# A decoder layer on one core: the twelve sign-weight loads move from SyncE's queue to ScalarE's, under new orders for all engines

## What is computed

```python
# causal self-attention, 16 heads of width 32
Q, K, V = X @ Wq.T + bq, X @ Wk.T + bk, X @ Wv.T + bv
attn = softmax(where(causal, Q @ K.T * scale, -inf))
x = layernorm(x + (attn @ V) @ Wo.T + bo)
# cross-attention: the rows of x are mixed by an attention of ctx with itself
q, k = ctx @ Wxq.T + bxq, ctx @ Wxk.T + bxk
x = layernorm(x + x @ softmax(q @ k.T).T)
# ternary feed-forward, hidden width 2048
xq = round(127 / max|n(x)| * n(x)) * max|n(x)| / 127     # n: row normalisation
x = layernorm(x + (silu(xq @ sign(W_g).T) * (xq @ sign(W_u).T)) @ sign(W_d).T)
```

## Time and profile before

| what | us |
|---|---|
| median of 3 runs (646.59 to 647.51) | 647.17 |
| span of the profiled execution | 649.9 |
| PE busy | 610.3 (94%) |
| DVE busy | 527.2 (81%) |
| ACT busy | 417.9 (64%) |
| POOL busy | 340.8 (52%) |
| chain that ended last: PE's share | 62% |

### The profile page before, as it was taken

How to read it: one execution, slowest core, us unless ns; L and a number is a source line. 1 busy time by engine, 2 the same in 40 slices (tenths; PEclk the granted TensorE clock), 3 DMA queues, 4 the chain that set the end, 5 groups by cost and what they waited for, 6 DMA issues and landing times.

```text
span 649.9 us, 14332 instructions
## 1 busy us (share of the span) xinstructions
PE 610.3 (94%) x5356; PEld 417.1 (64%) x5356; DVE 527.2 (81%) x1376; ACT 417.9 (64%) x789; POOL 340.8 (52%) x472
## 2 busy tenths in 40 slices
PE   5995798998999999999899999999999999999996
PEld 4572476665766677757466666777776667676563
DVE  5786575996998976669999998758998899897775
ACT  6838597954667886635574795754467568963341
POOL 9236554421663784435882465533577337736253
PEclk9998697998999999999999999999999999999999
DMA  9885512062011210151200030111222010010000
GB/s 313 276 284 163 197 68 50 24 234 89 14 32 43 75 35 2 25 163 38 61 11 2 17 115 3 26 26 66 50 50 50 18 50 3 2 37 30 1 33 33
DMA packets 31461, 45.63 MB, mean 70 GB/s; under 512 B 5664, under 2 KB 22560, under 8 KB 29856
## 3 DMA queue, kind: packets, MB, share of 16 engines
q1 hardware_dynamic: 30848, 44.20, 21.8%
q10 hardware_dynamic: 544, 0.52, 0.2%
HBM read 27.79 MB, written 4.19 MB: 49 GB/s over the span
## 4 chain that ended last, share of the span: by engine, by line
PE 62%; DVE 11%; ACT 6%; issue 4%; SPq 1%; POOL 1%; DMA 1%; POOLq 0%; ACTq 0%; DVEq 0%
PE ps_b L672 20%; PE ps_b L840 15%; PE ps_b L855 14%; PE ps_b L767 4%; PE ps_b L746 3%; PE ps_b L776 2%; DVE ps_b L1118 1%; PE ps_b L729 1%; ACT ph L949 1%; PE ps_b L725 1%; SPq L634 1%; ACT ps_b L950 1%; DVE qk L1100 1%; ACT p L936 1%; DVE dg L1211 1%
## 5 line engine op out<-in xcount | busy, mean ns | idle before, releaser
L1118 DVE CUSTOM_DVE_ANT_0 ps_b<-ps_b,future 128x256 f32<-128x256 f32 (+3 forms) x256 | 118.9, 515 | 17.7 <-PE ps_b L725 11.3
L1319 POOL TENSOR_TENSOR ph<-p,ph 128x512 f16<-128x512 f32 x96 | 110.3, 1165 | 42.2 <-ACT ph L873 41.5
L840 PE MATMUL ps_b<-xqT,sg 128*128 128x256 f16 x1024 | 124.3, 275 | 3.8 <-ACT xqT L873 2.4
L855 PE MATMUL ps_b<-sd,hp 128*128 128x512 fp8e4 x512 | 119.1, 379 | 0.0
L1315 POOL TENSOR_TENSOR hp<-gt,hp 128x512 f16<-128x512 f32 x64 | 74.1, 1164 | 82.7 <-ACT hp L873 82.7
L840 PEld LDWEIGHTS ps_b<-xqT,sg 128*128 128x128 fp8e4 x1024 | 99.4, 98 | 22.5 <-issue 4.1
L1277 POOL TENSOR_SCALAR_AFFINE_SELECT p<-p 128x256 f32<-128x256 f32 (+1 forms) x96 | 46.5, 494 | 77.8 <-ACT p L936 77.0
L672 PE MATMUL ps_b<-xhl,wh 128*128 128x256 f16 x480 | 82.4, 273 | 0.0
L855 PEld LDWEIGHTS ps_b<-sd,hp 128*128 128x128 f16 x512 | 48.7, 98 | 51.1 <-POOL hp L1315 0.3
L1028 ACT ACTIVATE gt<-gt 128x512 f32<-128x512 f32 x64 | 40.1, 629 | 47.0 <-DVE gt L1226 46.9
L936 ACT ACTIVATE p<-ps_b 128x512 f32<-128x512 f32 x96 | 54.2, 598 | 19.3 <-PE ps_b L746 18.5
(11 more groups left out here) (135 smaller groups left out, 1208.2 us busy)
## 6 DMA issues: line engine op xcount, KB each, us to landing
st<-qk SPq DMA_DIRECT2D x192, 64.0 KB, 2.0
hp<-in_sgT_dram SPq DMA_DIRECT2D x6, 1024.0 KB, 7.2
gt<-in_sgT_dram SPq DMA_DIRECT2D x6, 1024.0 KB, 6.5
rows<-in_x_dram SPq DMA_DIRECT2D x8, 512.0 KB, 3.7
out_dram<-rows SPq DMA_DIRECT2D x16, 256.0 KB, 2.0
xin<-in_xT_dram SPq DMA_DIRECT2D x14, 256.0 KB, 3.5
e<-in_ctxT_dram SPq DMA_DIRECT2D x4, 512.0 KB, 4.1
hp<-in_wT_dram SPq DMA_DIRECT2D x4, 256.0 KB, 4.4
```

Source lines behind the costliest of these rows:

```text
L840: ins = pe.matmul(ps[:, a * HALF:(a + 1) * HALF], sg[:, ("gg", "uu").index(name), c, ht * P:(ht + 1) * P], xqT[:, c, :], start=c == 0, sto ...
L855: ins = pe.matmul(ps[:, :], hp[:, (UNITS * s + n) % HP_SLOTS, h, a, t * P:(t + 1) * P], sd[:, ht, :], start=ht == h == 0, stop=ht == HT - ...
L1118: ins = dve.tensor_tensor_reduce(scores, scores, future[:, S - width:S], 1.0, -3e38, ALU.add, ALU.max, tops[:, g // 2, j:j + 1, g % 2, qt ...
L1319: pool.tensor_tensor(out_, in_, hi, ALU.subtract).then_inc(signal, 1)
```

## The change

It does five things. `load_signs` leaves the sync engine and is issued by ScalarE, with the same waits (`w_lo` for the first two, then the sign of piece i - 2), now held by ScalarE. All five tables and the banks are written anew. Words of single steps take the place of pairs. GpSimd's `rms_scale` waits for the root that `row_scale` just made. The functions are otherwise as they were.

```diff
-            def load_signs(i):
-                if i < 2:
-                    sp.wait_ge(w_lo, 4 * (i + 1))
-                else:
-                    sp.wait_ge(signs, i - 1)
-                sp.dma_start(stage[i % 2], sgT[i]).then_inc(weight_in[i % 2], 16)
...
+            def load_signs(i):
+                if i < 2:
+                    wait_for(act, w_lo, 4 * (i + 1))
+                else:
+                    wait_for(act, signs, i - 1)
+                act.dma_start(stage[i % 2], sgT[i]).then_inc(weight_in[i % 2], 16)
...
             def rms_scale(s, t):
                 tile = 2 * (s % 2) + t
                 root = rstd[:, 1, tile:tile + 1]
+                wait(pool, ln_rstd[1], s, t + 1)
```

Two lines of the tables for scale, on TensorE, where `mx1.0.0.0` is the first product that needs `sk1.0.0.*`:

```diff
-st0.1.2.2@0 qk1.0.3@3 mx1.0.0.0@5 en0.3@4 pv0.1.1.0@6 pv0.1.1.1@6 pv0.1.1.2@6 pv0.1.1.3@6 st0.1.2.3@0 st0.1.2.4@7
...
+st0.1.2.5@6 op0.0.0@5 mx1.0.0.1@0 mx1.0.0.0@4 pv0.1.2.0@2 st0.1.2.3@7 tx0.0.0@5 op0.0.1@4 pv0.1.2.1@2 ta0.2@5
```

More of the change, by code:

```diff
@@ L130 @@
[L130 to L144, removed]
@@ new lines @@
+pv0.1.1.3@4 st0.1.3.0@0 st0.1.3.2@1 st0.1.2.4@2 to0.0.1@7 st0.1.2.5@6 op0.0.0@5 mx1.0.0.1@0 mx1.0.0.0@4 pv0.1.2.0@2
+st0.1.2.3@7 tx0.0.0@5 op0.0.1@4 pv0.1.2.1@2 ta0.2@5 pv0.1.2.2@2 st0.1.3.3@6 tx0.0.1@4 ta0.3@7 pv0.1.2.3@2 st0.1.3.1@1
+st0.1.3.4@3 mx1.0.0.2@5 st0.1.3.6@0 st0.1.3.5@1 xm0.0.0@7 xm0.0.1@6 pv0.1.3.0@7 pv0.1.3.1@7 pv0.1.3.2@7 pv0.1.3.3@7
+va1.0.0@6 to0.1.0@7 to0.1.1@0 mx1.0.1.1@1 mx1.0.3.0@2 va1.0.1@4 mx1.0.2.1@6 op0.1.0@7 ib0@4 mx1.0.1.0@0 op0.1.1@5
+mx1.0.2.0@1 mx1.0.1.2@0 mx1.0.2.2@4 tq0.0.0@7 qk1.1.0@3 qk1.1.1@1 nm1.0.0@3 tq0.0.1@2 tx0.1.1@4 mx1.0.3.2@6
@@ new lines @@
+mx1.0.3.1@7 tx0.1.0@0 uu0.0.1@2 gg0.0.0@3 uu0.0.0@7 xm0.1.0@4 st1.0.0.0@3 xm0.1.1@6 mx1.1.0.1@3 mx1.1.0.4@4
+mx1.1.0.0@7 gg0.0.2@0 gg0.0.1@6 mx1.1.0.2@1 uu0.0.3@5 uu0.0.2@3 qk1.1.2@7 mx1.1.0.3@0 st1.0.0.2@6 gg0.0.3@1 cp1.0@3
+cp1.1@4 mx1.1.0.5@7 st1.0.0.1@0 st1.0.1.0@2 gg0.0.5@3 gg0.0.4@7 mx1.1.0.6@4 mx1.1.1.0@6 gg0.0.6@2 mx1.1.0.7@5
+mx1.1.1.1@0 uu0.0.4@1 en1.0@5 uu0.0.5@6 pv1.0.0.0@0 dn0.0.1.0@7 mx1.1.1.2@5 st1.0.1.1@4 en1.1@1 pv1.0.0.1@0
+pv1.0.0.2@0 pv1.0.0.3@0 ta1.0@5 st1.0.1.2@4 qk1.1.3@3 dn0.0.0.0@5 ta1.1@0 mx1.1.1.3@4 mx1.1.1.4@1 mx1.1.1.6@6
@@ new lines @@
+dn0.0.0.1@5 pv1.0.1.0@0 dn0.0.0.2@5 gg0.0.7@2 uu0.0.6@1 ib1@4 mx1.1.1.5@3 pv1.0.1.1@0 pv1.0.1.2@0 pv1.0.1.3@0
+mx1.1.2.0@1 nm1.0.1@4 dn0.0.1.1@7 tq0.1.1@0 uu0.0.7@4 tq0.1.0@2 mx1.1.2.1@6 mx1.1.1.7@3 dn0.0.1.2@7 st1.0.2.0@1
+st1.0.2.1@0 nm1.1.0@6 en1.2@2 mx1.1.3.3@1 mx1.1.2.2@3 en1.3@6 mx1.1.2.3@0 st1.0.2.2@4 dn0.0.0.3@5 gg0.1.0@0 ta1.2@4
+st1.0.3.1@6 mx1.1.2.5@5 st1.1.0.2@2 mx1.1.2.4@3 dn0.0.1.3@7 pv1.0.2.0@4 pv1.0.2.1@4 pv1.0.2.2@4 pv1.0.2.3@4 uu0.1.0@2
+gg0.1.1@7 va1.1.0@3 ta1.3@2 st1.0.3.0@5 mx1.1.2.6@4 uu0.1.1@0 st1.0.3.2@3 mx1.1.2.7@5 mx1.1.3.0@7 va1.1.1@2 gg0.1.2@7
@@ new lines @@
+mx1.1.3.1@5 st1.1.0.0@4 st1.1.0.1@0 st1.1.0.4@3 mx1.1.3.2@2 uu0.1.3@6 gg0.1.3@5 pv1.0.3.0@2 pv1.0.3.1@2 pv1.0.3.2@2
+pv1.0.3.3@2 gg0.1.4@1 uu0.1.2@3 st1.1.1.0@7 gg0.1.5@0 mx1.1.3.4@3 st1.1.0.6@7 dn0.1.1.0@5 st1.1.0.3@3 st1.1.0.5@2
+st1.1.1.2@6 dn0.1.0.0@4 dn0.1.1.1@5 st1.1.1.4@2 mx1.1.3.7@1 st1.1.1.3@3 dn0.1.0.1@4 st1.1.1.1@6 pv1.1.0.0@7
+pv1.1.0.1@7 pv1.1.0.2@7 pv1.1.0.3@7 mx1.1.3.6@2 mx1.1.3.5@6 qk2.0.0@0 nm1.1.1@1 uu0.1.4@3 st1.1.1.6@7 st1.1.1.5@2
+pv1.1.1.0@6 pv1.1.1.1@6 to1.0.0@1 gg0.1.6@0 uu0.1.5@2 st1.1.2.2@3 st1.1.2.0@7 pv1.1.1.2@6 pv1.1.1.3@6 st1.1.2.3@2
@@ new lines @@
+mx0.1.2.2 mx0.1.2.3 ov0.0.0 ov0.0.1 mx0.1.2.4 mx0.1.2.5 ez0.2 mx0.1.2.6 mx0.1.2.7 mx0.1.3.0 mx0.1.3.1 mx0.1.3.2
+mx0.1.3.3 mx0.1.3.4 mx0.1.3.5 ov0.0.2 lo0.1.0.2 lo0.1.0.3 lo0.1.0.5 mx0.1.3.6 mx0.1.3.7 lo0.1.0.6 ov0.0.3 nm0.1.1
+qk1.0.1 ta0.1 lo0.1.1.2 ov0.1.0 lo0.1.1.3 lo0.1.1.5 lo0.1.1.6 lo0.1.2.2 en0.3 qk1.0.2 qk1.0.3 ez0.3 to0.0.0 to0.0.1
+ov0.1.1 op0.0.0 mx1.0.0.0 mx1.0.0.1 os0.0.0 lo0.1.2.3 tx0.0.0 lo0.1.2.5 op0.0.1 lo0.1.2.6 lo0.1.3.2 ta0.2 os0.0.1
+ta0.3 mx1.0.0.2 tx0.0.1 lo0.1.3.3 ov0.1.2 xm0.0.0 lo0.1.3.5 lo0.1.3.6 xm0.0.1 n10.0.0 ov0.1.3 n20.0.0 to0.1.0 va1.0.0
@@ new lines @@
+mx1.1.1.4 hw0.0.6 n20.1.1 ga0.0.7 hd0.0.6 mx1.1.1.5 mx1.1.1.6 ov1.0.1 nm1.0.1 hw0.0.7 hd0.0.7 mx1.1.1.7 mx1.1.2.0
+mx1.1.2.1 nm1.1.0 en1.2 mx1.1.2.2 mx1.1.2.3 ez1.2 en1.3 dn0.0.0 ga0.1.0 ez1.3 ta1.2 mx1.1.2.4 lo1.1.0.2 dn0.0.1
+hw0.1.0 ga0.1.1 mx1.1.2.5 hd0.1.0 ov1.0.2 hw0.1.1 va1.1.0 ta1.3 hd0.1.1 mx1.1.2.6 mx1.1.2.7 mx1.1.3.0 va1.1.1 ga0.1.2
+mx1.1.3.1 mx1.1.3.2 mx1.1.3.3 ga0.1.3 hw0.1.2 hw0.1.3 hd0.1.2 hd0.1.3 mx1.1.3.4 ov1.0.3 ga0.1.4 lo1.1.0.3 ga0.1.5
+lo1.1.0.5 hw0.1.4 hw0.1.5 lo1.1.0.6 lo1.1.1.2 mx1.1.3.5 mx1.1.3.6 mx1.1.3.7 lo1.1.1.3 ov1.1.0 qk2.0.0 nm1.1.1 hd0.1.4
```

412 lines of the change are left out of this document (199 added, 213 removed).

## The result

The kernel after takes 662.76 us (661.03 to 664.74, 4 runs) against 646.88 beside it: 1.0235 times as long, interval 1.0207 to 1.0262. That is **slower by 15.9 us**, where 640.0 was predicted and 632 to 651 was the range. The profiled execution has a span of 659.3 against 649.9. The time of an execution is its span plus 1.7 to 1.8 us.

A forecast was written before the change was run, and what follows sets the result against it. TensorE was taken to bind behind 160 us and ScalarE to tie the middle together. The terms -3.7 - 3.5 + 0 = -7.2 gave a span of 642.7, the median 2.7 below: 640.0 us, range 632 to 651.

The forecast's parts named there:

- first mark: Start of the second step's score maxima; claimed to move by +4.6 us, from 52.0 to 56.6.
- Part 1: First weights: with four key chunks ahead of the first query weights, TensorE starts at 9.7, 2.4 us late.
- Part 2: ScalarE between the first projections: output weights split before cross weights, TensorE waits 3.3 us at the context; net +2.2.
- Part 3: ScalarE from first mark to first normalisation: 62.7 us work, 5.5 of 12.0 idle left; normalisation at 125.8, -3.7.
- Part 4: Last signs before the feed-forward: each load directly follows the sign freeing its buffer; -3.5 us, bounds 0 and -5.5.
- Part 5: The rest, behind 160 us: some 7 us idle is all that can be saved; taken as 0, 3 either way.
- ScalarE's mark: Start of ScalarE's first normalisation of step 0; claimed to move from 129.5 to 125.8 us, -3.7.
- What bounds the kernel: Opening step: TensorE binds behind 160 us with some 7 us idle; ScalarE ties the middle, working 64.49 of 76.5 us.
- ScalarE is held by its own loads: Rival, chance 0.20: sign pieces wait for loads on ScalarE, first mark 9 us late; +2.7 in all, about 650.
- Only the issuer: Rival, chance 0.12: the move changes only who issues and every wait keeps its length; about 647.3.

The follow-up runs named there:

- head_before: Kernel after with everything up to the first gate product of step 0 in the orders and banks of before (sign loads on SyncE): 657.2 us (1.0152).
- after_two_back: Kernel after with sign loads 0 and 1 back on SyncE's queue behind the small loads, loads 2 to 11 still on ScalarE: 660.3 us (1.0197).
- after_half: Kernel after with sign loads 2 to 11 halved in bytes: 650.7 us (1.0052).
- last_three: Kernel before with only sign loads 9, 10 and 11 issued by ScalarE, each behind the piece that frees its buffer: 649.4 us (1.0011).
- signs_refit2: Kernel before, all loads on SyncE: sign piece 7 earlier, load 9 between batch 1's two dozen stacks, piece 11 behind the last flip: 646.8 us (0.9984).
- loads_timed: Kernel before with sign loads 2 to 11 issued by ScalarE at about the times SyncE issued them: 651.6 us (1.0053).
- queue_alone: Kernel before, its orders and banks kept, with all twelve sign loads issued by ScalarE: 658.7 us (1.0181).

## Why the prediction was wrong, point by point

The forecast and the two traces, part by part (us against before):

| stretch | forecast | measured |
|---|---|---|
| to the first mark (parts 1 and 2) | +4.6 | +4.9 |
| to ScalarE's first normalisation (the first three parts) | -3.7 | +2.5 |
| from there to the gate's first products, their clock included (part 4) | -3.5 | +0.9 |
| from there to the end (part 5) | 0 | +6.0 |
| span | -7.2 | +9.4 |

Part 4's +0.9 is 5.1 (156.81 for 151.72) less the 2.5 ahead of it and less the 1.7 of the clock; part 5 is 502.5 for 498.2, with the same 1.7 added. The other 6.5 us of the 15.9 are the distances of the traced executions from their medians. In head_before, the same program up to the gate, ScalarE's mark comes 2.5 us earlier than in the trace of before, so some of it lies there.

- **What bounds the kernel**: right that behind 160 us only TensorE counts and that there is nothing to gain. Wrong to conclude that there is little to lose.
- **Part 1**: right. +2.4 was taken, the first matmul came at 9.62 for 9.7.
- **Part 2**: right in place, size (3.07 for 3.3) and reason. The terms as they stand add up to 31.4 and not to 30.8; the cross weights were ready at 30.3. The output weights landed at 23.6 (24.1 was kept). The rule cited there, that DMA engines take turns between queues ("DMA: Bandwidth & Descriptors" of the Trainium skill), agrees with the landings: with load 0 beside them the output weights took 13.6 us from their issue, with both loads behind them in one queue (after_two_back) 8.8. The cross weights, which had no price, took 15.0 us and were there at 26.6; ScalarE came to them only at 28.4, so this cost nothing here. But they are the sign of what was left out: "ahead" was counted for one load, and the small transfers that shared the time with the loads were not.
- **The first mark**: 56.96 for 56.6. Right, and of little use: the wait of 3.04 us stands right behind it, so the first exponential began 9 us late (62.44 for 53.4), not 4.6.
- **Part 3**: this is the step that failed. The sum had ScalarE's work, its issues and its idle time, and for the loads only their own landing, 6.7 us. It had no term for what a load on a second queue does to the transfers of the first, and so left 5.5 us of idle time. The work was right: 60.8 us without the issues, as forecast. The idle time was 11.9 us: 74.11 less 60.81, and less four issues of 0.34. ScalarE waited for TensorE (4.42, 2.89 and 1.55 us the longest), and TensorE for stacks. The mark came at 132.01 for 125.8.

```profile
57.90:132.01 74.11, 61.87 (x676) 42.65 (x677) 54.26 (x154) 60.81 (x118) 41.78 (x56) 0.88 0.31 93
57.70:124.73 67.03, 57.83 (x676) 41.22 (x677) 54.38 (x154) 60.74 (x119) 41.69 (x56) 0.92 0.26 73
```

  The second row is after_half: half the bytes take 7.0 us of idle time away. Halving them in the kernel before took 2.3 in the same stretch (12.0 to 9.7, the latter from 51.96 to 125.20 us), so some 4.7 of the 7.0 are the missing term; that the mark with half the bytes (124.73) is near the forecast for full ones is in part luck.
- **Part 4**: the gap ahead of the gate went and the clock is full there, as said, and the 3.5 us did not come. A wait of 2.80 us for stacks took its place 18 us earlier; last_three shows the exchange alone (1.93 for 3.59, no gain). signs_refit2 keeps a gap of 1.67 at full clock, and its time is 0.9984 of before's (0.9962 to 1.0005): that much is worth 2.5 us at most. The bound of -5.5 for this part had no row behind it.
- **Part 5**: 0 with 3 either way was too narrow; it was 6.0, of which 4.4 us are new idle time behind 160 us, shown by head_before to belong to the orders. "What they can lose has no row" was said and then not taken into the range.
- **The rivals**: *ScalarE is held by its own loads* had the right first 60 us (exponentials 9 late) and a wrong mechanism: in after the trace has no wait of ScalarE for a sign load, and none of its twelve issues took over 0.36 us; loads_timed leaves at most 1.5 to 5.4 us for ScalarE's own share. *Only the issuer* fell with queue_alone. The Trainium skill's sentence that issuing from several engines saves only the sequencer's issue time ("Trainium Kernel Development and Optimization", key constraints) was read as "nothing else changes". Queue_alone and loads_timed show that something else does: which transfers are in flight together.
- **The range**: its upper end came from one rival with two small waits. One number of the earlier trace rows would have asked the right question: the DMA engines are 0.88 busy from 7.3 to 50.7 us. The stacks issued from 19 to 45 us landed in 2.8 us before and in 4.4 after.
